# GpSimd's scatters placed behind the score products, key masks per batch, and one TensorE signal per round of the tile loop

## The reference, cut to what matters

```python
scores = jnp.einsum('bhqd,bhkd->bhqk', q, k) / jnp.sqrt(hd)      # 16 heads of 8
attn = jax.nn.softmax(scores, axis=-1)
o = jnp.einsum('bhqk,bhkd->bhqd', attn, v)
x = _layernorm(x + o @ wo.T + bo, ln1_g, ln1_b)
flat_e = g_idx * 2 + e_idx_local                 # one expert of 8 per token
h = relu(x @ w1[flat_e] + b1[flat_e])            # 128 -> 256
y = h @ w2[flat_e] + b2[flat_e]                  # 256 -> 128
x = _layernorm(x + p * y, ln2_g, ln2_b)          # p: the gate's probability
```

## Time and profile before

| | |
|---|---|
| median of three runs | 565.12 us (563.15 to 565.46) |
| the profiled execution | 566.35 us, its span 564.5 us |
| busy: TensorE | 493.2 us (87%) |
| busy: VectorE | 425.3 us (75%) |
| busy: ScalarE | 375.2 us (66%) |
| busy: GpSimd | 290.9 us (52%) |

### The profile page before, as it was taken

How to read it: one execution, slowest core, us unless ns; L and a number is a source line. 1 busy time by engine, 2 the same in 40 slices (tenths; PEclk the granted TensorE clock), 3 DMA queues, 4 the chain that set the end, 5 groups by cost and what they waited for, 6 DMA issues and landing times. The chain is left out here.

```text
span 564.5 us, 14903 instructions
## 1 busy us (share of the span) xinstructions
PE 493.2 (87%) x4887; PEld 330.2 (58%) x4887; DVE 425.3 (75%) x1188; ACT 375.2 (66%) x1144; POOL 290.9 (52%) x515
## 2 busy tenths in 40 slices
PE   5998899999999999999789999988987777688781
PEld 3665566667767777765345565554554455566660
DVE  3589988888888888998466788777778768656562
ACT  3557688888888877778456677656656546467550
POOL 0587653222222222045344568877686446746564
PEclk9999999999999999999999999999999988979876
DMA  8700999999999000403100000101141053243300
GB/s 348 292 3 1 283 274 272 281 276 274 282 274 269 27 0 12 138 1 150 37 3 3 1 3 21 50 20 50 40 169 49 31 140 91 80 120 108 103 30 8
DMA packets 49865, 65.13 MB, mean 115 GB/s; under 512 B 2536, under 2 KB 45557, under 8 KB 48646
## 3 DMA queue, kind: packets, MB, share of 16 engines
q1 hardware_dynamic: 47014, 57.91, 36.8%
q0 software_dynamic: 2784, 6.37, 3.2%
HBM read 20.53 MB, written 44.20 MB: 115 GB/s over the span
## 5 line engine op out<-in xcount | busy, mean ns | idle before, releaser
L1626 DVE TENSOR_REDUCE nm<-SC 128x8 f32<-128x1024 f32 x64 | 75.3, 1219 | 28.3 <-PE SC L1119 27.8
L2143 ACT ACTIVATE room_p<-ST 128x512 f32<-128x512 f32 (+1 forms) x96 | 64.1, 740 | 47.1 <-PE ST L1138 44.7
L1522 DVE TENSOR_REDUCE room_w<-SC 128x512 f32<-128x2048 f32 x32 | 73.0, 2281 | 1.0 <-PE SC L948 1.0
L615 POOL TENSOR_TENSOR spread<-parts,units 128x48 bf16<-128x48 bf16 x32 | 8.8, 276 | 122.2 <-DVE parts L1497 122.2
L2050 ACT ACTIVATE room_w<-room_w,shift 128x128 f32<-128x128 f32 x128 | 49.7, 390 | 19.0 <-DVE shift L1531 18.9
L815 POOL DMA_INDIRECT out<-room_v,id_r x39 | 38.9, 997 | 26.2 <-DVE room_v L1964 16.6
L2041 ACT ACTIVATE room_w<-ST,cv 128x128 f32<-128x128 f32 x128 | 36.4, 366 | 18.5 <-PE ST L963 18.4
L963 PEld LDWEIGHTS ST<-room_w 128*128 128x128 f32 x256 | 33.1, 191 | 15.3 <-issue 13.0
L2059 ACT ACTIVATE room_w<-room_w,inv 128x128 f32<-128x128 f32 x128 | 41.0, 407 | 0.1
L1158 PE MATMUL SC<-room_p,room_w 128*32 128x128 f32 x1024 | 36.3, 280 | 5.3 <-DVE room_w L1650 2.0
L717 POOL DMA_INDIRECT sorted_rows<-room_w,slot_i x32 | 33.4, 1044 | 13.6 <-issue 11.2
(11 more groups left out here) (306 smaller groups left out, 1344.5 us busy)
## 6 DMA issues: line engine op xcount, KB each, us to landing
sorted_rows<-w SPq DMA_DIRECT2D x8, 4290.0 KB, 41.1
room_v<-sorted_rows SPq DMA_DIRECT2D x39, 130.0 KB, 2.0
x_t<-xT SPq DMA_DIRECT2D x2, 1024.0 KB, 8.2
ctx_t<-adj SPq DMA_DIRECT2D x1, 2048.0 KB, 17.0
biased_rows<-room_w SPq DMA_DIRECT2D x2, 1024.0 KB, 4.5
room_w<-biased_rows SPq DMA_DIRECT2D x8, 256.0 KB, 3.3
room_w<-mask SPq DMA_DIRECT2D x1, 1536.0 KB
w<-weights SPq DMA_DIRECT2D x1, 1356.0 KB, 8.9
```

Of the source, the lines that this page charges most:

```text
L1522: dve.tensor_reduce(logit[:, :, :], SC[:, :, :].rearrange("p b (i m) -> p b m i", i=TYPES), AX_X, ALU.max)\
L1626: dve.tensor_reduce(nm[:, v % 2, 2 * PER_R * pair:2 * PER_R * (pair + 1)], SC[:, 2 * pair:2 * pair + 2, :].rearrange("p r (i n) -> p (r i) ...
L2143: act.activation(ex[:, v % 2, first:last, :], ST[:, first:last, :], ACT.Exp)\
```

## The change

1. Head loop, GpSimd: a round waits for `s_mm` (from round 12 on for both pairs), and then starts with the `scatter`; batch n of a group now goes out in round b = n. The first batch of group 4 goes at the end of round 27, the other three in rounds 28 and 29 (the last at the round's end), the last groups as before. `rows_x1` is cut in two: `rows_scaled` at b = 2 ahead of `top_parts`, `rows_moved` at b = 3 behind it.
2. Key masks: in each round, behind `top_parts`, one instruction writes all four copies of one batch (`k_m[:, g % 2, :, cols]`). TensorE waits at every `scores` for the mask of its batch (`keys_of`). Both query masks of GpSimd are at b = 1.
3. Tile loop: TensorE signals once per round, `step_mm`, on the last product of the round (the transpose; in the closing rounds the first layer, then the second). VectorE's L1948 and ScalarE's L2230 and L2237 wait for the round in which their input was made; ScalarE's two waits for older products are dropped.

```diff
@@ GpSimd, head loop
-            def mask_keys(g, heads):
-
+            def mask_keys(g, b):
+
+                cols = slice(b * N, (b + 1) * N)
                 pool.wait_ge(S("key_ready"), g + 1)
-                for i in heads:
-                    pool.tensor_tensor(k_m[:, g % 2, i, :], k_s[:, g % 2, :],
-                                       C("hmask")[:, i:i + 1].broadcast_to([128, GT]), ALU.mult)\
-                        .then_inc(S("km_ready"), 1)
+                pool.tensor_tensor(k_m[:, g % 2, :, cols],
+                                   k_s[:, g % 2, cols].unsqueeze(1).broadcast_to([128, PER_R, N]),
+                                   C("hmask").unsqueeze(2).broadcast_to([128, PER_R, N]), ALU.mult)\
+                    .then_inc(S("km_ready"), 1)
...
                 if batch(u + LEAD):
-                    pool.wait_ge(S("s_mm"), 2 * (u + LEAD) + 1)
-                if b == 0 and more and nxt > 0:
-                    mask_keys(nxt, (0, 1))
+                    pool.wait_ge(S("s_mm"), 2 * (u + LEAD) + (2 if u >= GB * 3 else 1))
+                if GB * 3 <= u < B - GB:
+                    scatter(norm - 1, b)
+                elif B - GB <= u < B - 2:
+                    scatter(norm - 1, b + 1)
                 if b == 0 and normed and norm < G - 2:
                     norm1_power(norm)
-                if b == 1 and more and nxt > 0:
-                    mask_keys(nxt, (2, 3))
-                    mask_queries(nxt, 0)
                 if b == 2 and normed:
-                    rows_x1(norm)
-                if b == 3 and more and nxt > 0:
-                    mask_queries(nxt, 1)
-                if normed and (u == B - 2 or b == 3 and u < B - 2):
-                    row_id(norm, 0)
+                    rows_scaled(norm)
                 if batch(u + LEAD):
                     top_parts(u + LEAD)
+                if normed and (u == B - 2 or b == 3 and u < B - 2):
+                    rows_moved(norm)
+                    row_id(norm, 0)
+                if more and nxt > 0:
+                    mask_keys(nxt, b)
+                if b == 1 and more and nxt > 0:
+                    mask_queries(nxt, 0)
+                    mask_queries(nxt, 1)
...
-                elif b == 3 and normed and u < B - 2:
+                if u == B - GB - 1:
                     scatter(norm, 0)
-                if b < GB - 1 and GB * 3 <= u < B - 2:
-                    scatter(norm - 1, b + 1)
                 if u == B - 3:
                     scatter(norm - 1, 3)
@@ TensorE, scores
+            return PER_R if v < GB else PER_R + v - GB + 1     # keys_of(v)
...
-                    pe.wait_ge(S("km_ready"), PER_R * (g + 1))
+                pe.wait_ge(S("km_ready"), keys_of(v))
@@ TensorE, tile loop
-                    mm.then_inc(S("y_mm"), 1)
+                    if k >= SLOTS + 2:
+                        mm.then_inc(S("step_mm"), 1)
...
-                    mm.then_inc(S("ht_mm"), 1)
+                    if k >= SLOTS:
+                        mm.then_inc(S("step_mm"), 1)
...
-                    pe.transpose(XT[k % 2], tile_s[:, k % RING, 0:D], C("ident")).then_inc(S("xt_mm"), 1)
+                    pe.transpose(XT[k % 2], tile_s[:, k % RING, 0:D], C("ident")).then_inc(S("step_mm"), 1)
@@ VectorE and ScalarE, tile loop
-                    dve.wait_ge(S("y_mm"), fresh + 1)
+                    dve.wait_ge(S("step_mm"), second_at(fresh) + 1)
...
-                    act.wait_ge(S("xt_mm"), t + 1)
-                    if t >= 2:
-                        act.wait_ge(S("ht_mm"), t - 1)
+                    act.wait_ge(S("step_mm"), t + 1)
...
-                    act.wait_ge(S("ht_mm"), t + 1)
-                    if t >= 2:
-                        act.wait_ge(S("y_mm"), t - 1)
+                    act.wait_ge(S("step_mm"), first_at(t) + 1)
```

More of the change, by code:

```diff
@@ L351, in build, with first_at, second_at @@
         HBANK = [ST[:, 0, :], SC[:, 0, :]]
+        def first_at(t):
+            return t + 2
+        def second_at(t):
+            return t + 4
         def fillers(t):
@@ L394, in group, with keys_of @@
             return (g + back, b, 0 <= g + back < G)
+        def keys_of(v):
+            return PER_R if v < GB else PER_R + v - GB + 1
         def batch(v):
@@ L693, in norm1_power, with rows_scaled, rows_moved @@
                 pool.tensor_tensor(rstd[:, :], ve[:, :], C("half"), ALU.pow).then_inc(S("rstd_ready"), 1)
-            def rows_x1(p):
+            def rows_scaled(p):
                 pool.wait_ge(S("xn_ready"), p + 1)
+                pool.tensor_tensor(x1_g[:, :, :], xn[:, :, :], R("ln1g").unsqueeze(1).broadcast_to([128, GB, D]),
+                                   ALU.mult).then_inc(S("x1g_ready"), 1)
+            def rows_moved(p):
                 bc = lambda n: R(n).unsqueeze(1).broadcast_to([128, GB, D])
-                pool.tensor_tensor(x1_g[:, :, :], xn[:, :, :], bc("ln1g"), ALU.mult).then_inc(S("x1g_ready"), 1)
                 pool.wait_ge(S("x1g_ready"), p + 1)
@@ L789, in rest @@
                     norm1_power(G - 1)
-                    rows_x1(G - 2)
+                    rows_scaled(G - 2)
+                    rows_moved(G - 2)
                 if k == 2:
@@ L1348, in _ @@
                 rest(k)
-                t = k - 4
+                t = k - second_at(0)
                 if 0 <= t < SLOTS:
@@ L1363, in _ @@
                                        w2_s[:, bass.ds(e * FF + f * D, D)], start=False, stop=(f == 1))
-                    mm.then_inc(S("y_mm"), 1)
+                    if k >= SLOTS + 2:
+                        mm.then_inc(S("step_mm"), 1)
                 if k == 5:
                     ranks(k)
-                t = k - 2
+                t = k - first_at(0)
                 if 0 <= t < SLOTS:
```

## The result

The changed kernel took 571.12 us (median of four runs, 570.15 to 572.32); the kernel before took 565.29 beside it. The ratio is 1.0096, with a 95% interval of 1.0062 to 1.0131. The forecast was 555.5 us with a range of 544 to 562: the time lies outside it, and on the other side of the kernel before.

The account below looks back on a forecast made before the run. TensorE was taken to bound the head loop, with scatters over round ends adding 2.8 us per four rounds from round 16. 566.35 - 9.3 (head loop) - 0 (tile loop) = 557.0, less 1.2 for the median: 555.8, stated 555.5 us, range 544 to 562.

Parts of the forecast that it names:

- What bounds the kernel: Head loop: TensorE at 97% up to round 15, then scatters over a round's end add 2.8 us per four rounds.
- Part 1, the scatter's place: Head loop: a scatter behind the score products no longer lies over the round's end and delays exponentials; -9.3 us.
- Part 2, does GpSimd fit: Head loop: GpSimd needs 20.5 us of a 21.7 us slot per four rounds; its late steps cost nothing.
- TensorE's further wait per round: Head loop: TensorE's added wait ahead of the score products costs nothing, 1.2 us at most.
- Part 3, one signal per round: Tile loop: nearly 78 of 117 TensorE signals removed, VectorE's L1948 0.56 us later in a free round; 0 taken.
- the bounds of +5.6 and -15: Tile loop: 10 stalls each 0.56 us longer, +5.6 us; half of the ScalarE and VectorE waits gone, -15 us.
- B: Head loop: GpSimd too full, one scatter in two over a round's end again, half of 9.3 lost; 560.5 us, chance 0.11.
- C: Head loop: late scatters hold L1158's 32 dense products as they held L1138; no gain, 565 us, chance 0.05.
- D: Tile loop: pace follows latency, VectorE's later start paid every round, 39 x 0.56 = 21.8 us; 577.6 us, chance 0.08.
- The signs: Head loop: groups 21.7 to 22.1 us, exponentials within 0.15, scatters 0.6 to 2 behind score products, ScalarE's waiting under 14.

Follow-up runs that it names:

- single fills: Changed kernel with GpSimd's key and query masks replaced by one constant fill each of the same regions, mask products left out: 560.82 us, 0.9883.
- the power ahead: Kernel before with the scatters moved and the first norm's power ahead of the round's wait, masks as before: 560.69 us, 0.9898; again 558.97 us, 0.9898.
- the kernel with early masks: Changed kernel with its masks ahead of the parts of the maxima instead of behind them, same instructions and TensorE waits: 565.11 us, 0.9988.
- spread query masks: Kernel before with scatters moved, the first norm's power ahead of the round's wait, first query mask moved from b = 1 to b = 2: 539.53 us, 1.0053.

## Why the prediction was wrong

Between the traces of both kernels on one chip the difference lies in few places. On the 566 kind (563.2 to 569.0 us of span): rounds 8 to 11 +4.3 (26.01 against 21.67), rounds 12 to 27 -0.2 (95.01, 95.24), round 28 +2.5 (9.15, 6.66), the rest, up to round 7 and from round 29 on, -0.8. On the 536 kind (538.3 to 550.5): +3.1, +7.3, +1.7 and +0.1.

Not all of this is the masks' work. Round 10 of the changed kernel took 7.93 us in its first trace and 9.07 in the second, where the granted clock was 0.84 and TensorE 6.75 us busy for 5.42; here are both:

```profile
330.25:338.18 7.93, 5.42 (x97) 3.41 (x89) 7.76 (x15) 3.76 (x9) 5.36 (x9) 1.00 0.00 1
329.26:338.33 9.07, 6.75 (x97) 3.92 (x89) 8.67 (x19) 3.80 (x9) 5.59 (x9) 0.84 0.01 3
```

In both TensorE had waited 2.2 us for the maxima. And round 28, before and after, differs in the clock as well:

```profile
434.95:441.60 6.65, 4.54 (x85) 2.66 (x76) 5.97 (x19) 2.83 (x6) 3.23 (x7) 1.00 0.07 22
438.40:447.43 9.03, 5.97 (x87) 3.64 (x77) 7.18 (x21) 2.88 (x6) 6.62 (x12) 0.81 0.19 60
```

It took 8.75 us at 0.80 with single fills, where no mask reads, so its excess isn't the masks' reading. TensorE had waited 2.28 us for the maxima there in the changed kernel, 1.85 with fills and 0.78 before. The kernel before on the 536 kind has such a round 28 too (8.24 us at 0.79).

- **What bounds the kernel: right for the chip of the profile.** The 2.8 us per four rounds are signals held by scatters. Where nothing is held, the same kernel has 87.41 us for rounds 12 to 27 instead of 95.24, so 7.8 was there to be gained; the prediction had 8.4 for rounds 16 to 27 and 0.2 for the four ahead.
- **Part 1, the scatter's place: right mechanism, gain too large.** Scatters alone brought 2.1 of the 8.6 us, and 5.5 with the power ahead (95.2 to 89.7, in both its runs). With single fills, on the 566 kind, the same place brought nearly all of it (87.2), with GpSimd emptier by half of each mask. What is missing goes with steps of GpSimd that come late: 3.4 us with the power, and 2.3 with the query mask that holds L1727 (the second share is argued from the rows, no run took that hold away alone).
- **Part 2, does GpSimd fit: the step that failed.** The prediction asked who waits for the late masks and found nobody, and concluded "I cost them at nothing; that cover is gone when GpSimd falls 2.5 us behind". Its sum for GpSimd was sound: a key mask took 1.046 us for 1.03, and GpSimd's busy time is 292.3 us for 290.9. What was never costed is what a mask does to VectorE while it runs. In the kernel before, their cover was the row maxima from PSUM; behind the parts they meet the gate's steps. That turned 0.16 us steps into 0.7 to 1.2 and cost 7.6 us in rounds 12 to 27 (94.8 against 87.2 with fills) and 3.1 more in rounds 8 to 11, where there was nothing to gain (24.8 against 21.7, both at a clock of 1.00). The hold could be seen ahead of the result: L1725 in round 13 of the kernel before. Lateness has a price of its own as well: the power, late behind the scatter, held VectorE's gate for 1.3 us per group.
- **TensorE's further wait per round: right.** In the changed kernel L1157 to L1138 in the same group take 0.22 us (348.71 to 348.93), as L1138 to L1119 did, and the kernel with early masks has all these waits and 21.67 us in rounds 8 to 11.
- **Part 3, one signal per round: right.** 1.0008 alone; 558.95 against 558.97 on top of the best version. From the first second-layer product to the end it is 92.6 us before, 93.4 after, and the bounds of +5.6 and -15 were both far off. On the 536 kind the whole loop took 74.3 and 73.7.
- **The rivals.** B (GpSimd too full, 560.5) has at most a share in the kernels with early masks, which lie 1.3 and 0.6 us per four rounds above the fills (92.3 and 89.4 against 87.2). In the first TensorE does wait for a late query mask; in the second a hold by the rows is in it, and less work for GpSimd gave nothing. The changed kernel's 2 us come from another mechanism. C is refuted by the fills, with the scatters at the same place, and by the two kinds of chip: rounds 12 to 27 of the changed kernel take 94.8 and 95.0 us where signals are held and 94.7 where they aren't. D forecast slower, by the tile loop; the loop didn't change. The mechanism that decided was on no list.
- **The signs.** Groups were at 23.6 and not 21.7 to 22.1. Others came as they were to come if the forecast was right: scatters started 0.85 to 1.55 us behind the score products in rounds 12 to 27, and exponentials 0.09 us behind the last L1157 product (349.11 to 349.20); ScalarE's waiting for it fell from 21.4 to 14.6 us. They show the scatters' part alone. Key masks were not over 1.3 us. None of the signs named looked at VectorE's busy time, which shows it in one line of the page.

What stays open: why the two kinds of chip differ (the second is one chip), and why the granted clock fell in round 10 of one trace of the changed kernel and not in the two others; with the fall rounds 8 to 11 took 26.0 us, without it 24.8. The version with the power first was timed on the 566 kind alone; a kernel like it, with spread query masks, was 0.5% slower than before on the other kind, where there is nothing held to be gained.

## What to carry to other kernels

Before an instruction is moved, list what runs beside it in its new place on the engine that shares its access to memory, and not only who waits for it: a mask that is off every path can stretch a chain of small two-operand steps more than fivefold (0.69 us to 3.81 for the four of round 9). Then look at what else stands behind it in its own queue. And measure on more than one chip where a stall depends on how a signal is delivered: the stall that this change set out to remove is 7.8 us of rounds 12 to 27 on one kind and not there on the other, and the same change cost 1% and 2.9%.

## What the runs showed of the hardware

- GpSimd's masks of 128x512 (1.04 us) held VectorE's TENSOR_TENSOR and SCALAR_TENSOR_TENSOR steps with both inputs in SBUF until they ended (all five of each of L1751, L1753 and L1755 that met one), and also a CAST with one input (L1768, 0.67 us for 0.21 in the kernel before). The rows' instructions (L710, L718, 1.27 us) did the same, to L1758 (1.16 us, in one round) and to a TENSOR_SCALAR with one input (L1685, 0.69 us for 0.17; five of its six met L718, one a key mask). Each held step ended 0.02 to 0.06 us behind the GpSimd instruction. Reductions, norm statistics and steps with an input in PSUM were not held (L1749 0.19, L1682 0.16, L1671 0.29). The Trainium skill (same page and section) names casts and tensor_scalar as able to enter a mode that uses both ports; the trace agrees. Fills didn't hold a two-operand step (0.16 and 0.19 us), which is the half of the rule that no row of before showed; one did hold a TENSOR_SCALAR with one input (0.55 us).
- GpSimd's indirect transfers did not hold VectorE's small steps (L1732 and L1734 of the kernel before, 0.16 and 0.19 us beside a transfer, four times each; one CAST beside a transfer, L1747 at 429.12, took 0.36 for 0.17). On three chips, with the kernel before at 566 to 568 us, they hold TensorE's signals; on one, with it at 536 to 537 us, they don't.
- The start of the head loop varies by itself: in one trace of the kernel with `step_mm` alone the granted clock was 0.77 on average from 275 to 281 us, so partly at the lower of its two levels (1.2 and 2.4 GHz), and round 8 began 3.3 us late, where the kernel before had 1.00. What two traces differ by ahead of round 2 is no price of the change.
